# First-pass maxima of a causal attention: the mask moved into the contraction, self scores apart, fewer fills in setup

## What is computed

```python
h = layernorm(x) * (1 + ca) + sa
x = x + ga * attention(h)
h = layernorm(x) * (1 + cb) + sb
x = x + gb * experts(h)          # top 2 of 8, silu gated
```

```python
std_logits = q @ k.T * scale
bias = incidence * decay ** (tq - tk) * (tk < tq) * bias_scale
logits = where(tq < tk, -inf, std_logits + bias)
attn = softmax(logits) @ v
```

## Time and profile before

| | us |
|---|---|
| median of 3 runs | 1110.35 |
| lowest, highest | 1106.92, 1112.86 |
| profiled execution, its own time | 1111.9 |
| span of the profile (first to last instruction) | 1110.2 |
| PE busy, share of the span | 935.1 (84%) |
| POOL busy | 811.72 (73%) |
| DVE busy | 775.47 (70%) |
| ACT busy | 721.62 (65%) |

### The profile page before, as it was taken

How to read it: one execution, slowest core, us unless ns; L and a number is a source line. 1 busy time by engine, 2 the same in 40 slices (tenths; PEclk the granted TensorE clock), 3 DMA queues, 4 the chain that set the end, 5 groups by cost and what they waited for, 6 DMA issues and landing times. The chain is left out here.

```text
span 1110.2 us, 30824 instructions
## 1 busy us (share of the span) xinstructions
PE 935.1 (84%) x9473; PEld 742.2 (67%) x9473; DVE 775.5 (70%) x2067; ACT 721.6 (65%) x1612; POOL 811.7 (73%) x1352
## 2 busy tenths in 40 slices
PE   2346899889999899998999989998872799999967
PEld 2335677767777777777777777776652688888852
DVE  8576668777777777777777777777746466555536
ACT  2435678887778877888787887876562455555520
POOL 8366668888888888888888888887435366666644
PEclk9997999999999999999999999998985899999989
DMA  7336556565666656666566665655411353333339
GB/s 189 114 110 161 150 139 172 152 178 137 168 159 158 172 147 160 161 158 173 143 163 159 153 178 146 163 156 157 118 44 49 79 168 93 91 91 91 83 138 357
DMA packets 233854, 160.39 MB, mean 144 GB/s; under 512 B 57376, under 2 KB 220512, under 8 KB 233568
## 3 DMA queue, kind: packets, MB, share of 16 engines
q1 hardware_dynamic: 222416, 133.77, 46.0%
q0 software_dynamic: 8448, 17.45, 5.1%
q10 hardware_dynamic: 2832, 7.20, 1.7%
HBM read 81.38 MB, written 76.19 MB: 142 GB/s over the span
## 5 line engine op out<-in xcount | busy, mean ns | idle before, releaser
L919 DVE TENSOR_REDUCE peak<-pre 128x6 f32<-128x768 f32 x256 | 244.5, 955 | 116.4 <-PE pre L759 113.5
L1151 ACT ACTIVATE PT<-sc 128x768 f32<-128x768 f32 x256 | 204.6, 799 | 35.3 <-PE sc L746 32.9
L950 DVE TENSOR_TENSOR sc<-sc,decay 128x512 f32<-128x512 f32 x256 | 177.5, 693 | 30.4 <-PE sc L730 25.3
L1637 POOL DMA_INDIRECT yab<-y_out,xt x136 | 131.4, 966 | 82.8 <-issue 63.4
L1359 POOL DMA_INDIRECT xg<-stage,slot_i x128 | 130.9, 1022 | 62.9 <-issue 26.8
L759 PE MATMUL pre<-causal,identb 128*128 128x256 bf16 x512 | 144.7, 283 | 0.0
L758 PE MATMUL pre<-KT,queries 84*128 84x256 bf16 x512 | 143.5, 280 | 0.0
L757 PE MATMUL pre<-KT,queries 84*128 84x128 bf16 x512 | 116.5, 228 | 20.4 <-DMA queries<-line_rows 12.6
L1591 DVE TENSOR_TENSOR hid<-silu,up 128x256 f32<-128x256 f32 x136 | 57.3, 421 | 82.0 <-ACT silu L1545 82.0
L743 PE MATMUL sc<-queries,KT 99*128 99x128 bf16 x512 | 101.6, 223 | 13.2 <-issue 6.8
L1545 ACT ACTIVATE silu<-up 128x256 f32<-128x256 f32 x136 | 52.2, 384 | 88.4 <-PE up L1481 88.4
(11 more groups left out here) (279 smaller groups left out, 2731.9 us busy)
## 6 DMA issues: line engine op xcount, KB each, us to landing
line_rows<-line_part SPq DMA_DIRECT2D x64, 216.0 KB
dim_rows<-dim_part SPq DMA_DIRECT2D x64, 192.0 KB, 2.1
KT<-dim_rows SPq DMA_DIRECT2D x64, 192.0 KB
queries<-dim_rows SPq DMA_DIRECT2D x64, 192.0 KB
line_rows<-line_part SPq DMA_DIRECT2D x64, 144.0 KB
KI<-line_rows SPq DMA_DIRECT2D x64, 144.0 KB
QI<-line_rows SPq DMA_DIRECT2D x64, 144.0 KB
xt<-xg SPq DMA_DIRECT2D x136, 65.0 KB, 1.9
```

The costliest lines, as they stand in the source:

```text
L919: nc.vector.reduce_max(peak[half][:, i:i + 2, 0:3], pre[:, :, 0:3 * P].rearrange("p n (g k) -> p n g k", g=3), AX.X)\
L950: nc.vector.tensor_tensor(seeded(p), seeded(p), decay[:, 2 * p:2 * p + 2, :].unsqueeze(2).broadcast_to([P, 2, NT, P]), ALU.mult).then_inc( ...
L1151: nc.scalar.activation(PT[p % 4][:], sc[:, window], ACT.Exp).then_inc(exped.sem, 1)
L1637: nc.gpsimd.indirect_dma_start(yab, bass.IndirectOffsetOnAxis(xt[r][:, D:D + 1].bitcast(i32), 0), y_out[r % 8][:], None).then_inc(y_sent[r ...
```

## The change

The first pass gets tiles of its own, KB and QB: 64 constant mask rows and under them the 48 rows of dimensions, loaded a second time from DRAM. A diagonal block is one matmul over these 112 rows; the block of the first keys and second queries is one over the 84 rows of KT and QF. KB and QB have one copy, so loading them waits until the first pass of the batch before has used that half. The mask rows hide an odd token from itself, so scores of tokens with themselves are made apart: DVE multiplies queries and keys (in the memory of attnT), the job "self" sums them by head on PE, and DVE copies the sums beside the maxima, which are kept for three batches. The peak rows move from 96 to 84. In setup the fills of KT and QF cover only what the loads leave open. The tile pads shares memory with KB and QB and is filled by POOL after the loop.

```diff
-PEAK0 = 96
+PEAK0 = DIMS + LINES
+PRE = MR + DIMS
-    (6, 0, "back", -2, 1), (6, 1, "max0", 1, 0),
+    (6, 0, "back", -2, 1), (6, 1, "max0", 1, 0), (6, 2, "self", 3, 1),
-        pads = sb(whole, "pads", [P, 16, ROW])
-        causal = a("causal", [P, P], bf16)
+        first_rows = a("first_rows", [P, 2, H, T], bf16)
+        KB, QB = (first_rows[:, n] for n in range(2))
+        pads = first_rows[:]...bitcast(fp32)[:, 0:16 * ROW]...
+        head_of = a("head_of", [P, H])
...
 setup, POOL
+                nc.gpsimd.memset(query_mask[0][:], MASK)
+                step(nc.gpsimd.memset(key_mask[0][:], 1.0))
+                nc.gpsimd.affine_select(out=key_mask[1][:], ...).then_inc(key_mask_ok, 1)
...
-                step(nc.gpsimd.memset(v["pads"][:], 0.0))
-                step(nc.gpsimd.iota(v["pads"][:, :, D:D + 1].bitcast(i32), ...))
-                step(nc.gpsimd.memset(mask0[:], 0.0))
-                step(nc.gpsimd.affine_select(out=mask1[:], in_=mask0[:], ...))
-                nc.gpsimd.tensor_copy(v["causal"][:], mask1[:])
...
-                    step(nc.gpsimd.memset(v["KT"][m][64:96].rearrange("p h t -> p (h t)").bitcast(u32), 0))
-                    step(nc.gpsimd.memset(v["KT"][m][96:P].rearrange("p h t -> p (h t)").bitcast(u32), ones_pair))
+                    step(nc.gpsimd.memset(v["KT"][m][64:96].rearrange("p h t -> p (h t)").bitcast(u32), ones_pair))
+                    step(nc.gpsimd.memset(pairs(v["KT"][m])[0:PEAK0, :, P // 2:P], 0))
 setup, ACT
+                act.wait_ge(query_mask_ok, 1)
+                nc.scalar.activation(v["QB"][0:MR]..., query_mask[2][:]..., ACT.Copy)
 setup, DVE
                 for m in range(2):
-                    nc.vector.memset(v["KT"][m][32:64]...bitcast(u32), 0)
-                    nc.vector.memset(v["QF"][m][32:64]...bitcast(u32), 0)
-                    nc.vector.memset(v["QF"][m][64:96]...bitcast(u32), 0)
+                    nc.vector.memset(pairs(v["QF"][m])[0:PEAK0, :, 0:P // 2], 0)
...
+                dve.wait_ge(key_mask_ok, 1)
+                for tile in ("KI", "KB"):
+                    nc.vector.tensor_copy(v[tile][0:MR]..., key_mask[1][:]...)
+                dve.wait_ge(ident_ok, 1)
+                nc.vector.reduce_sum(v["head_of"][:], ident[:].rearrange("p (d h) -> p h d", h=H), AX.X)
                 dve.wait_ge(wT_ok, 1)
...
-                dve.wait_ge(key_mask_ok, 1)
-                nc.vector.tensor_copy(v["KI"][0:MR]..., key_mask[1][:]...)
 attend
-        peak = [a(f"peak{n}", [P, 8, 4]) for n in range(2)]
+        peak = [a(f"peak{n}", [P, H, NT, 3]) for n in range(3)]
+        peak_top = [a(f"peak_top{n}", [P, 8, NT]) for n in range(2)]
+        own_part = attnT
 SP, load_rows
-                    hold(pre_ready, jb - 1, 4 * half + 1)
+                    hold(pre_ready, jb - 1, 4 * half + 4)
+                    for kq, tile in ((0, KB), (1, QB)):
+                        sp.dma_start(tile[MR:PRE, heads, :], dim_rows[jb % 3][kq, :, heads, :]).then_inc(done, 16)
 SP, after the loop
+                sp.wait_ge(pads_made, 2)
                 sp.dma_start(xg[E * CAP:XROWS, :]..., pads[:, 8:16, :]).then_inc(padded, 16)
 PE, prescores
-                        nc.tensor.matmul(pre[:, n, 0:P], QF[par][0:DIMS + LINES, h, 0:P], KT[par][0:DIMS + LINES, h, 0:P], start=True, stop=False)
-                        nc.tensor.matmul(pre[:, n, P:3 * P], QF[par][0:DIMS + LINES, h, P:T], KT[par][0:DIMS + LINES, h, :], start=False, stop=False)
-                        last = nc.tensor.matmul(diagonal(pre, n), identb[:], causal[:]..., start=False, stop=True)
+                        nc.tensor.matmul(pre[:, n, 0:P], QB[0:PRE, h, first], KB[0:PRE, h, first], start=True, stop=True)
+                        nc.tensor.matmul(pre[:, n, P:T], QF[par][0:PEAK0, h, second], KT[par][0:PEAK0, h, first], start=True, stop=True)
+                        last = nc.tensor.matmul(pre[:, n, T:3 * P], QB[0:PRE, h, second], KB[0:PRE, h, second], start=True, stop=True)
 PE, job
+                    elif name == "self":
+                        wait(pe, own_ready, jb)
+                        for t in range(NT):
+                            last = nc.tensor.matmul(B[:, t * H:(t + 1) * H], own_part[:, t * P:(t + 1) * P], head_of[:], start=True, stop=True)
 DVE, body: the maxima go to peak[pb % 3], the last of a half to peak_top[half]
 DVE, bank_copies
+                    if p == 7 and live(b + 3):
+                        jb = b + 3
+                        wait(dve, ready["self"], jb)
+                        wait(dve, peaked, jb - 3, 2)
+                        own = bank[BANK["self"]][:, 0:NT * H].rearrange("p (t h) -> p h t", h=H)
+                        nc.vector.tensor_copy(peak[jb % 3]..., own).then_inc(used["self"].sem, 1)
 DVE, extras
                     if p == 4 and live(b + 3):
                         jb = b + 3
+                        wait(dve, used["kq"], jb)
+                        wait(dve, ready["self"], jb - 1)
+                        wait(dve, ready["out"], jb - 4)
+                        nc.vector.tensor_tensor(own_part[:], dim_val[:, 0, :], dim_val[:, 1, :], ALU.mult).then_inc(own_ready.sem, 1)
 ACT: the copy of kq waits for own_ready of the batch before, that of attnT for "self" of batch jb + 3
 ACT, after the loop
+                act.wait_ge(pads_made, 2)
 POOL, after the loop
                 iterations(pool, body)
+                wait(pool, pre_ready, NB - 1)
+                nc.gpsimd.memset(pads[:], 0.0).then_inc(pads_made, 1)
+                pool.wait_ge(pads_made, 1)
+                nc.gpsimd.iota(pads[:, :, D:D + 1].bitcast(i32), ...).then_inc(pads_made, 1)
                 wait(pool, scattered, NB - 1)
```

More of the change, by code:

```diff
@@ L194, in build @@
         QI = a("QI", [P, H, T], bf16)
+        first_rows = a("first_rows", [P, 2, H, T], bf16)
+        KB, QB = (first_rows[:, n] for n in range(2))
+        pads = first_rows[:].rearrange("p n h t -> p (n h t)").bitcast(fp32)[:, 0:16 * ROW].rearrange("p (n d) -> p n d", d=ROW)
+        head_of = a("head_of", [P, H])
         VP = [a(f"VP{n}", [P, NT, H, 32]) for n in range(2)]
@@ L365, in _ @@
                 nc.scalar.activation(lz[:], ez[:], ACT.Ln, bias=1.0).then_inc(ln_ok, 1)
+                act.wait_ge(query_mask_ok, 1)
+                nc.scalar.activation(v["QB"][0:MR].rearrange("p h (t q) -> p (h t) q", t=NT),
+                                     query_mask[2][:].unsqueeze(1).broadcast_to([MR, H * NT, P]), ACT.Copy)
                 act.wait_ge(ld_v, 64)
@@ L923, in body @@
                                 wait(dve, maxed, pb, 4 * half + 4)
-                                nc.vector.reduce_max(peak[half][:, :, 3], peak[half][:, :, 1:3], AX.X).then_inc(peaked.sem, 1)
+                                wait(dve, peak_step, pb - 1, 2 * half + 2)
+                                nc.vector.reduce_max(peak_top[half][:], mine[:, 8 * half:8 * half + 8], AX.X).then_inc(peaked.sem, 1)
                         extras(b, par, p)
@@ L934, in bank_copies @@
                 def bank_copies(b, p):
+                    if p == 7 and live(b + 3):
[3 more added lines that the diff above has]
+                        own = bank[BANK["self"]][:, 0:NT * H].rearrange("p (t h) -> p h t", h=H)
+                        nc.vector.tensor_copy(peak[jb % 3][:].rearrange("p h t k -> p h (t k)")[:, :, 1:6:4], own)\
+                          .then_inc(used["self"].sem, 1)
                     if p == 3 and live(b - 3):
@@ L1056, in _ @@
                 nc.vector.memset(three_halves[:], 1.5)
+                for n in range(3):
+                    nc.vector.memset(peak[n][:, :, 0, 0:1], MASK)
                 for n in range(2):
@@ L1103, in evacuate @@
                         wait(act, dim_rested, jb - 1)
+                        wait(act, own_ready, jb - 1)
                         for n in range(2):
@@ L1125, in evacuate @@
                     elif name == "attnT":
+                        wait(act, ready["self"], min(jb + 3, NB - 1))
                         nc.scalar.activation(attnT[:], B[:, 0:T], ACT.Copy).then_inc(done, 1)
@@ L1172, in body @@
                         for name, jb in [job for place in range(3) for job in jobs_at(b, p, place)]:
-                            if name[:-1] != "head" and name not in ("route", "rank", "norm2") and (name != "v" or b < 0):
+                            if name[:-1] != "head" and name not in ("route", "rank", "self", "norm2") and (name != "v" or b < 0):
                                 evacuate(name, jb, jb % 2)
@@ L1322, in split_peaks @@
                     wait(pool, ready[f"max{half}"], jb - 1)
-                    top_q = peak[half][:, :, 0:4:3].rearrange("p h t -> p t h")
+                    top_q = peak_top[half][:].rearrange("p h t -> p t h")
                     settle(pool, pool_settled)
```

57 lines of the change are left out of this document (26 added, 31 removed).

## The result

The changed kernel takes 1246.2 us (median of 4 runs, 1244.3 to 1256.9), the kernel before 1109.1: a ratio of 1.125 (1.119 to 1.131). The forecast was 1119, its range ended at 1138.

A forecast was written before the change was run, and what follows sets the result against it. The prediction took POOL to set the loop's period. Setup -2, first iterations +2, steady loop +2.5, last iterations +0.5 and end of attention +5.5 summed to +8.5 us: 1119 us beside the median, range 1103 to 1138.

The forecast's parts named there:

- +2.5 us: Attention loop, 26 steady iterations: 0.1 us an iteration, between a gain of 2 us and a loss of 0.5.
- +2 and +0.5: First three and last two loop iterations: later rows against PE's saving, ranges -5 to +5 and -3 to +3 us.
- Setup: Before the loop: fewer DVE fills against added mask copies and stalls beside POOL's fills, -2 us (-6 to -1).
- End of attention: After the last scatter: POOL fills the pads and SP stores them, delaying the expert tiles, +5.5 us (4.5 to 7).
- Later landing: Row loads in the loop: each half lands 1.5 us later through added transfers, between 0.8 and 2.4 us.
- The cover: Row loads in the loop: PE's 1.21 us stand hides half 1's lateness; half 0 has only PE's 1.9 us saving.
- rival 4: First pass of slots 1 and 5: row loads become the bound, about 1 us an iteration, 1142 us; chance 15%.
- PE's saving: Loop: net 1.45 us less PE work an iteration, which becomes idle time on PE and moves nothing.
- POOL's limit: Steady loop: POOL sets the 23.05 us period, with 20.15 us busy and the rest fixed gaps between its instructions.
- rival 5: Loop: DVE's product holds up POOL by 0.35 us, 26 times, 9 us in place of 2.5, 1125 us; chance 12%.

The follow-up runs named there:

- e8: Changed kernel with SP's dims stores behind peaks and lines, rows of half 1 ahead of its peaks, and pads filled in iteration 33: 1288.0 us.
- e9: Changed kernel, but after batch 0 each KB and QB load carries one head of eight (24 KB for 192 KB), same issues: 1155.4 us, one run.
- e1: Changed kernel with only SP's order changed: rows of half 1 ahead of dims stores and peaks, dimension rows of half 0 ahead of line stores: 1148.7 us.
- e12: Kernel before with SP issuing half 1's rows first (1105.9 us), plus the change's setup part, peak rows at 84, pads filled in iteration 33: 1114.0 us.
- e6: Kernel before, SP order kept, with the small operations that split the maxima on DVE in place of POOL: 1135.4 us.
- e3: Changed kernel without the scores of tokens with themselves (DVE product, job self, DVE copy and their waits left out): 1245.4 us.
- e5: Kernel before with SP's order changed: rows of half 1 ahead of its peaks, dims stores behind peaks and lines: 1255.6 us.
- e4: Changed kernel with three more fp32 products of 384 columns on PE in slot 5, ahead of the wait for rows, results overwritten: 1226.5 us.
- e2: Kernel before with four more 192 KB transfers an iteration ahead of the rows, into a tile nobody reads; PE waits for them: 1258.1 us.

## Why the prediction was wrong

It failed in the loop: +2.5 us was forecast for 26 iterations and +118.5 came, +2 and +0.5 for the iterations ahead of and behind them and +16.0 and +5.4 came. The steps behind that are the cover of half 1, the size of the later landing, and the price of a stand. The terms for setup and for the end of attention held in kind.

- **Setup**, -2: measured -2.3. The stalls that kept it small are there: a copy of biases (L416) takes up to 3.55 us, where it took 1.03 before (L409). Right.
- **End of attention**, +5.5: measured 7.4, and 5.92 us from scatter to load with the pads early (e8). The mechanism is right, the term is 1.9 us too small. SP issued its last pad store 6.1 us behind the scatter's start (at 1001.39), where the forecast's steps give 5.8; by the semaphore records it took 5.0 us to land, where 3.3 was taken. The forecast's count ends 866.8 - 861 = 5.8 us later, of which it wrote 5.5.
- **Later landing**, 1.5 us a half: half 1's rows landed 9.29 us after max1 in place of 6.82, 2.5 us later, 0.9 of it in the issuing and 1.5 from the last issue to the landing. Half 0's came 3.0 later behind max0. Right in kind, with both parts (e9), but the term is 1.0 us too small for half 1, and both values lie above the upper end of its range, 2.4.
- **The cover**, the step that failed: "Half 1 has the 1.21 us stand of PE as cover". That stand is at the job head0 (L823 of the kernel before), which PE works behind the first pass of the same slot: in the iteration shown, first pass at 408.12, head0 at 410.05. What stands behind the user of a load can't hide the load's lateness. The slack of half 1 was 0.38 us (median), that of half 0, which the prediction took for the barer one, 0.67, and half 1 was the half in which every one of the 26 iterations of the changed kernel stood. Even 1.21 us would not have covered 2.5.
- **The price of a stand**, left out: rival 4 had the place and the sign, at 1 us an iteration and 1142 us; an iteration lost 4.55 (table: legs A and B up by 2.0 and 2.5). A stand is followed by some 10 us of half clock, and PE's slower leg B then delays the next maxima, peaks and rows: SP issues rows only behind the peaks, so the delay goes round. In e1, with the same work on PE, leg B was 16.03: 2.05 us less than in the changed kernel, which bounds what the lower clock took there. By itself, 6.8 us at half clock cost 2.2 us in e12 and 2.4 in e9. The row for it was in the trace of before, unread: 0.52 behind the stand of the earlier trace rows, and that iteration took 25.3 us from max1 to max1 (123.76 to 149.09), the one ahead of it 20.8 and the one behind 22.5.
- **PE's saving**: PE reached the first pass 0.44 us earlier in leg A and this moved nothing, as forecast; it only made the stand longer. POOL's limit was read half right: the shortest iterations of e9 and e12 lasted 22.9 us as before, but e6 shows another chain as long.
- **The product** (rival 5): without it, the time is the same (e3), and POOL's busy time did not rise with it (523.37 us in 26 iterations, 523.98 before, where rival 5 meant 9 more). It is not the cause here. In this loop POOL waited for others, so what the product costs where POOL sets the pace isn't shown.

## What to carry to other kernels

To price a later load, take the time from its issue to its first user in a steady iteration, and ask what lies between them in the user's own order; idle time behind the user is no cover. Where the issue itself waits for a result of that user, lateness goes round the loop, and a stand of TensorE is priced with the half-clock stretch that follows it in the same trace. The load's landing can be read directly, from the last update of the semaphore that its user waits for. An edit in a queue that several engines wait on is checked against every landing that others wait for, as the dims stores of e5 teach.

## What had not been expected of the hardware

- Giving PE useless work in place of part of a stand made the kernel faster by 20 us (e4), with the granted clock up from 0.81 to 0.93.
- Iterations with the same stands of PE lasted 2.2 us (e12) and 2.4 us (e9) longer with 6.8 us at half clock in them; a stand of 0.86 us was followed by such a stretch in one iteration of e9 and not in the one ahead of it.
- Two transfers of 192 KB a half, on DMA engines that were 0.61 busy, filled them at the moment that matters: a busy share of 1.08 by the profile in the stand, 297 GB/s behind it, with line stores on SP from 412.64 on, just behind the rows.
- Stands of quite different origin, for rows (after, e2) or for ACT behind a store (e5), ended at nearly the same period, 27.6 to 28.3 us an iteration.
